# First pair of heads on one core: projections woven with the feed-forward's last down products, Q's and K's rests formed by VectorE, the other element's layer norm spread

## The reference

```python
# feed-forward: silu gate, RMS norm, down product
h  = silu(gate) * up
hn = rms_norm(h)                       # x * rsqrt(mean(x*x) + eps)
x  = x + 0.5 * einsum('bsh,dh->bsd', hn, wq_p)
# attention over the layer norm of x
qkv = einsum('bsd,od->bso', layernorm(x), w_qkv)
q, k = rope(q), rope(k)                # x*cos + rotate_half(x)*sin
attn = softmax(einsum('bqhd,bkhd->bhqk', q, k) / sqrt(128))
x = x + einsum('bso,do->bsd', einsum('bhqk,bkhd->bqhd', attn, v), w_out)
```

## Time and profile before

| what | value |
|---|---|
| median of 3 runs | 1762.09 us (1761.56 to 1762.62) |
| the profiled execution's own time | 1760.51 us |
| its span | 1758.7 us |
| PE busy | 1645.4 us, 94% of the span |
| DVE busy | 1287.1 us, 73% |
| ACT busy | 1219.9 us, 69% |
| POOL busy | 1126.1 us, 64% |
| mean granted TensorE clock | 0.991 |

### The profile page before, as it was taken

One profiled execution on the slowest core, in us unless ns is written; L12 is line 12 of the kernel. 1 busy time (PEld: TensorE's weight loads), 2 busy tenths in 40 slices (PEclk: granted clock), 3 DMA queues, 4 the chain that ended last, 5 costly groups with the idle time before them and its releaser, 6 DMA issues.

```text
span 1758.7 us, 26693 instructions
## 1 busy us (share of the span) xinstructions
PE 1645.4 (94%) x9307; PEld 963.8 (55%) x9307; DVE 1287.1 (73%) x2427; ACT 1219.9 (69%) x1886; POOL 1126.1 (64%) x747
## 2 busy tenths in 40 slices
PE   0898789999999999999999999998999999899998
PEld 0565345555555555555555555554565565676565
DVE  7877657777777777767777777786687778886766
ACT  6655778888888888988988888874654443325432
POOL 0554768888888888888888878883763222653222
PEclk9999899999999999999999999999999999999999
DMA  8100567887888878889878788784001210000001
GB/s 284 49 1 19 101 115 144 139 138 144 150 150 146 147 140 154 148 135 164 144 136 152 130 145 151 128 137 89 0 1 58 64 40 1 1 1 28 28 10 48
DMA packets 580506, 174.03 MB, mean 99 GB/s; under 512 B 543243, under 2 KB 579350, under 8 KB 580246
## 3 DMA queue, kind: packets, MB, share of 16 engines
q1 hardware_dynamic: 580374, 172.33, 51.8%
HBM read 35.94 MB, written 2.10 MB: 22 GB/s over the span
## 4 chain that ended last, share of the span: by engine, by line
PE 73%; DVE 8%; POOL 2%; issue 2%; ACT 1%; SPq 0%; DMA 0%; DVEq 0%; POOLq 0%; ACTq 0%
PE banks L1789 23%; PE banks L1790 23%; PE banks L1791 23%; DVE X L1644 1%; POOL sq_sum L684 1%; DVE mo_h L1631 1%; DVE nmax L1463 1%; DVE x L1196 1%; PE banks L1887 1%; PE banks L1855 1%; PE banks L1888 1%; PE banks L1856 1%; PE banks L1939 0%; PE banks L1799 0%; PE banks L2100 0%
## 5 line engine op out<-in xcount | busy, mean ns | idle before, releaser
L737 POOL TENSOR_TENSOR Pl<-Pm,Ph 128x1024 f16<-128x1024 f32 x256 | 546.4, 2134 | 52.3 <-ACT Ph L962 51.3
L952 ACT ACTIVATE Pm<-banks,nbias,s_scale 128x1024 f32<-128x1024 f32 x256 | 308.0, 1203 | 135.9 <-DVE nbias L1465 135.7
L1463 DVE TENSOR_REDUCE nmax<-banks 128x1 f32<-128x1024 f32 x256 | 312.6, 1221 | 111.6 <-PE banks L1791 110.5
L962 ACT ACTIVATE Ph<-Pm 128x1024 f16<-128x1024 f32 x256 | 268.3, 1048 | 1.2
L716 POOL TENSOR_TENSOR rp_b<-rp_s,rope 128x512 f32<-128x512 f32 x128 | 162.8, 1272 | 150.9 <-ACT rp_s L929 150.9
L1502 DVE SCALAR_TENSOR_TENSOR X<-banks,rinv,X 128x256 f32<-128x256 f32 x256 | 112.7, 479 | 156.8 <-PE banks L1791 156.8
L790 POOL TENSOR_TENSOR mT_lo<-mo_h,mT_hi 128x512 f16<-128x512 f32 x72 | 83.7, 1162 | 214.2 <-ACT mT_hi L1064 213.9
L1789 PE MATMUL banks<-QK_hi 128*128 128x512 f16 x512 | 197.1, 385 | 6.8 <-DVE QK_lo L1539 2.7
L1789 PE MATMUL banks<-PT_hi,V_hi 128*128 128x512 f16 x512 | 194.9, 381 | 3.2 <-DMA PT_lo<-Pl 3.2
L1790 PE MATMUL banks<-QK_lo,QK_hi 128*128 128x512 f16 x512 | 195.5, 382 | 0.0
L1791 PE MATMUL banks<-QK_hi,QK_lo 128*128 128x512 f16 x512 | 195.5, 382 | 0.0
(11 more groups left out here) (240 smaller groups left out, 4136.4 us busy)
## 6 DMA issues: line engine op xcount, KB each, us to landing
moe_raw<-in_L_ffn_W SPq DMA_DIRECT2D x72, 128.0 KB, 2.3
w_all<-in_L_attn_w_qkv SPq DMA_DIRECT2D x3, 2048.0 KB, 16.5
a_raw<-in_L_attn_w_qkv SPq DMA_DIRECT2D x24, 256.0 KB, 3.1
PT_hi<-Ph SPq DMA_TRANSPOSE x256, 3.4
PT_lo<-Pl SPq DMA_TRANSPOSE x256, 3.4
raw_gu<-in_L_ffn_w_gate_up SPq DMA_DIRECT2D x2, 1024.0 KB, 7.3
X<-in_L_attn_x SPq DMA_DIRECT2D x2, 1024.0 KB, 13.1
o_raw<-in_L_attn_w_out SPq DMA_DIRECT2D x8, 256.0 KB, 3.4
```

The source lines that it names most:

```text
L737: nc.gpsimd.tensor_tensor(Pl[:, z % 4, :], Pm[:, k, :], Ph[:, z % 4, :], ALU.subtract).then_inc(pl_done.sem, 1)
L952: nc.scalar.activation(Pm[:, k, :], two_banks[z % 2][:], ACT.Exp, bias=nbias[:, z:z + 1], scale=s_scale[:], accum_out=rsum[:, z:z + 1]).th ...
L962: nc.scalar.activation(Ph[:, z % 4, :], Pm[:, (base * SLOTS + z) % 3, :], copy).then_inc(ph_done.sem, 1)
L1463: nc.vector.tensor_reduce(nmax[:, z:z + 1], two_banks[z % 2][:], AX, ALU.max, negate=True).then_inc(max_done.sem, 1)
```

## The change

TensorE no longer finishes the four last down products before the projections. `ffn(0, 0)` returns two functions, the last phase's down product j and its squares, and `attention` calls them in this order: down 0, projections 0 and 1, squares, projection 2, down 1, projection 3, values 0, down 2, values 1, down 3, the first half scores. The banks change with it (downs 7, 6, 7, 6, squares 6, values 1 and 2), the wait for element 0's second normalised half stands ahead of down 0, the second half score waits for the second value rest, and the sides 0 and 1 of the first pair wait for the adds of down 3 and down 2. VectorE does the adds between its rope instructions; VectorE and ScalarE mix the weight copies with the last feed-forward ones.

All of Q's and K's rests of the first pair for its own heads (numbers 3 to 7) move from GpSimd to VectorE: number 3 behind the maximum of slot 0, a side's rest two slots after it, behind that slot's maximum. The variances of element 1 move from before the first maximum into slots 0 and 1, GpSimd's roots into its slots 1 and 2, and the normalising goes by two tiles in slots 1 to 4. Some buffers get other places in SBUF, so that attention's Q, K and V can be written while the last down products still read their operands.

```diff
@@ -244,15 +245,15 @@
     place["at"] = phase0
-    PT_hi = sb("PT_hi", [P, 2, TT, HALF], fp16)
-    PT_lo = sb("PT_lo", [P, 2, TT, HALF], fp16)
+    Pl = sb("Pl", [P, 4, S], fp16)
+    place["at"] = hT_at
     QK_hi = sb("QK_hi", [P, 2, 2, S], fp16)
     QK_lo = sb("QK_lo", [P, 2, 2, S], fp16)
+    PT_hi = sb("PT_hi", [P, 2, TT, HALF], fp16)
     V_hi = sb("V_hi", [P, 2, TT, 2 * HD], fp16)
     V_lo = sb("V_lo", [P, 2, TT, 2 * HD], fp16)
+    PT_lo = sb("PT_lo", [P, 2, TT, HALF], fp16)
     Ph = sb("Ph", [P, 4, S], fp16)
-    Pl = sb("Pl", [P, 4, S], fp16)
-    rp_q = sb("rp_q", [P, 2, HALF], f32)
     place["at"] = max(place["at"], top_ffn)
@@ -300,7 +302,8 @@
     N_POOL_LO = len(POOL_LO)
-    END_BANKS = [(4, 6, 7, 5), (4, 2, 3, 5)]
+    END_BANKS = [(7, 6, 7, 6), (4, 2, 3, 5)]
+    END_SQUARES = [6, 5]
@@ -352,8 +355,8 @@
     SIDES["first"] = {
-        0: [Side("qk", 0, 4, 6, ("v", 0, 1))],
-        1: [Side("qk", 0, 5, 7, ("v", 0, 0))],
+        0: [Side("qk", 0, 4, 6, ("ffn", 0, 3))],
+        1: [Side("qk", 0, 5, 7, ("ffn", 0, 2))],
         2: [Side("qk", 0, 6, 6, ("qk", 0, 4))],
@@ -750,14 +753,16 @@
                             rope_sine(side.i, c)
+                    if body == "first" and s in (1, 2):
+                        rsqrt_ln(1, 1, s - 1)
                     if s:
...
                     if has_slots(body):
-                        if s == 0 and body == "first":
-                            rope_lo(3, of)
                         for side in sides_of(s - 3):
+                            if body == "first" and side.d == 0:
+                                continue
                             rope_lo(side.i, lambda sig, i, d=side.d: of(sig, i, d))
@@ -772,8 +777,6 @@
                     rope_sine(j, pre, PRE_QKO)
-                for half in range(NHALF):
-                    rsqrt_ln(1, 1, half)
                 attention_pair("first", 0)
@@ -901,12 +904,15 @@
                         ln_hi(0, l + 1, ht // 4)
-                hi(NS - 1)
-                square(NS - 1)
                 if f == 0:
-                    for i in range(3):
-                        weights_hi(W_ORDER[i], bank[i], w_psum.in_head(0, i + 1))
+                    weights_hi(W_ORDER[0], bank[0], w_psum.in_head(0, 1))
+                    hi(NS - 1)
+                    weights_hi(W_ORDER[1], bank[1], w_psum.in_head(0, 2))
+                    square(NS - 1)
+                    weights_hi(W_ORDER[2], bank[2], w_psum.in_head(0, 3))
                 else:
+                    hi(NS - 1)
+                    square(NS - 1)
                     expert_weights_hi(0)
@@ -1026,15 +1032,15 @@
                 rope_shift_step(1, bank[0], pre(qk_psum, 2))
-                values_hi(0, 0, bank[7], pre(v_psum, 1))
                 rope_hi(0, pre(rope_sum, 1), PRE_QKO)
-                rope_hi(1, pre(rope_sum, 2), PRE_QKO)
-                values_hi(0, 1, bank[6], pre(v_psum, 2))
                 act.wait_ge(rope_b.sem, pre(rope_b, 1))
                 rope_shift_step(2, bank[4], pre(qk_psum, 3))
+                rope_hi(1, pre(rope_sum, 2), PRE_QKO)
                 act.wait_ge(rope_b.sem, pre(rope_b, 2))
                 rope_shift_step(3, bank[5], pre(qk_psum, 4))
+                values_hi(0, 0, bank[1], pre(v_psum, 1))
                 rope_hi(2, pre(rope_sum, 3), PRE_QKO)
+                values_hi(0, 1, bank[2], pre(v_psum, 2))
                 attention_pair("first", 0)
@@ -1348,7 +1354,7 @@
                     tiles = slice(phase % NHALF * TPH, (phase % NHALF + 1) * TPH)
-                    nc.vector.tensor_scalar(ms4[:, tiles], bank[5][:, D:D + TPH], 4.0 / FF, 4 * RMS_EPS, ALU.mult, ALU.add).then_inc(ms_ready.sem, 1)
+                    nc.vector.tensor_scalar(ms4[:, tiles], bank[END_SQUARES[f] if phase == len(PHASES) - 1 else 5][:, D:D + TPH], 4.0 / FF, 4 * RMS_EPS, ALU.mult, ALU.add).then_inc(ms_ready.sem, 1)
@@ -1412,17 +1418,21 @@
                         late_scales()
+                if f == 0:
+                    weights_lo(W_ORDER[0], bank[0], w_hi_done.in_head(0, 1))
+                    lo(NS - 1)
+                    weights_lo(W_ORDER[1], bank[1], w_hi_done.in_head(0, 2))
+                    add(len(PHASES) - 2, 3)
+                    weights_lo(W_ORDER[2], bank[2], w_hi_done.in_head(0, 3))
+                    mean_squares(len(PHASES) - 1)
+                    return (lambda j: add(len(PHASES) - 1, j))
                 lo(NS - 1)
                 add(len(PHASES) - 2, 3)
-                if f == 0:
-                    for i in range(3):
-                        weights_lo(W_ORDER[i], bank[i], w_hi_done.in_head(0, i + 1))
-                else:
-                    expert_weights_lo(0)
+                expert_weights_lo(0)
                 mean_squares(len(PHASES) - 1)
                 for j in range(TPH):
                     add(len(PHASES) - 1, j)
-                    if f and j == 1:
+                    if j == 1:
                         expert_weights_lo(1)
@@ -1449,6 +1459,12 @@
                 nc.vector.tensor_tensor(rp_q[:, j % 2, :], src, rp_b[:, j % 2, :], ALU.add).then_inc(rope_sum.sem, 1)
+
+            def first_rope_lo(j):
+                k = (PRE_QKO if j < 4 else QKO)[j % 4]
+                part = (slice(None), j // 4, k // 2, slice(k % 2 * HALF, (k % 2 + 1) * HALF))
+                dve.wait_ge(qk_hi.sem, qk_hi.in_pair(0, j + 1))
+                nc.vector.tensor_tensor(QK_lo[part], rp_q[:, j % 2, :], QK_hi[part], ALU.subtract).then_inc(qk_lo.sem, 1)
@@ -1507,6 +1523,12 @@
                         maximum(s)
+                    if body == "first" and s == 0:
+                        first_rope_lo(3)
+                    if body == "first" and s >= 2:
+                        for side in SIDES["first"][s - 2]:
+                            if side.name == "qk" and side.d == 0:
+                                first_rope_lo(side.i)
                     if body == "tail" and block_done(s, body):
@@ -1521,41 +1543,37 @@
                             add_head(side)
-                    if body == "first" and s in (1, 4):
-                        ln_normalise(1, 1, (1, 4).index(s))
+                    if body == "first" and s < NHALF:
+                        ln_variance(1, 1, s)
+                    if body == "first" and 1 <= s <= 4:
+                        ln_normalise(1, 1, (s - 1) // 2, range((s - 1) % 2 * 2, (s - 1) % 2 * 2 + 2))
                     if body == "last" and s == 7:
...
-            def attention():
+            def attention(last_down):
                 def pre(sig, i):
                     return sig.in_pair(0, i)
-                def rope_lo(j):
-                    k = PRE_QKO[j]
-                    part = (slice(None), 0, k // 2, slice(k % 2 * HALF, (k % 2 + 1) * HALF))
-                    dve.wait_ge(qk_hi.sem, pre(qk_hi, j + 1))
-                    nc.vector.tensor_tensor(QK_lo[part], rp_q[:, j % 2, :], QK_hi[part], ALU.subtract).then_inc(qk_lo.sem, 1)
-
                 dve.wait_ge(rope_in.sem, 16)
                 rope_cos(0, bank[3], pre(rope_shift, 2), PRE_QKO)
+                last_down(0)
+                rope_add(0, bank[3], pre)
                 rope_cos(1, bank[0], pre(rope_shift, 4), PRE_QKO)
-                rope_add(0, bank[3], pre)
                 rope_add(1, bank[0], pre)
-                values_lo(0, 0, bank[7], pre(v_hi_done, 1))
-                rope_lo(0)
-                rope_lo(1)
+                first_rope_lo(0)
                 rope_cos(2, bank[4], pre(rope_shift, 6), PRE_QKO)
-                dve.wait_ge(qk_lo.sem, pre(qk_lo, 1))
+                last_down(1)
+                first_rope_lo(1)
                 rope_add(2, bank[4], pre)
-                rope_lo(2)
-                values_lo(0, 1, bank[6], pre(v_hi_done, 2))
                 rope_cos(3, bank[5], pre(rope_shift, 8), PRE_QKO)
-                dve.wait_ge(qk_lo.sem, pre(qk_lo, 2))
+                values_lo(0, 0, bank[1], pre(v_hi_done, 1))
+                first_rope_lo(2)
                 rope_add(3, bank[5], pre)
-                for half in range(NHALF):
-                    ln_variance(1, 1, half)
+                values_lo(0, 1, bank[2], pre(v_hi_done, 2))
+                for j in (2, 3):
+                    last_down(j)
                 attention_pair("first", 0)
@@ -1862,7 +1879,7 @@
                     for j in range(TPH):
-                        last = nc.tensor.matmul(bank[5][:, D + j:D + j + 1], sq_sum[:, phase % NHALF, (FT - 1) % 2, j * P:(j + 1) * P], ones,
+                        last = nc.tensor.matmul(bank[END_SQUARES[f] if phase == len(PHASES) - 1 else 5][:, D + j:D + j + 1], sq_sum[:, phase % NHALF, (FT - 1) % 2, j * P:(j + 1) * P], ones,
                                                 start=True, stop=True)
@@ -1871,11 +1888,9 @@
                         to = bank[END_BANKS[f][j]]
-                        if j == 1 and f == 0:
-                            x_ready(0, l + 1, 1)
-                    if n >= 2 and (phase < len(PHASES) - 1 or j == 0):
```

(39 more changed lines are left out.)

8 lines of the change are left out of this document (4 added, 4 removed).

## The result

Before: 1761.56 us, median of 17 runs (1759.53 to 1762.76). After: 1765.83 us, median of 17 runs (1763.24 to 1769.32), ratio 1.0028 with a 95% interval of [1.002, 1.0035]. The change makes the kernel slower by 4.3 us in the medians and 4.9 us by the ratio; +6.4 was forecast. The profiled execution took 1769.25 us, with a span of 1767.5 at a mean granted clock of 0.986 (before: 1758.7 at 0.991).

A forecast was written before the change was run, and what follows sets the result against it. TensorE bounds from 280 us; before, the first head pair's ring through the engines does. Head start 5.7 spent in slots of 39.2 (+0.7), plus contention 5.7: +6.4 us, 1768.5 on the median of 1762.09; range 1761.5 to 1770.5.

The forecast's parts named there:

- The head start (5.7 us): First pair: the weaving lets the first row maximum start at about 164.2 us against 169.94, 5.7 us earlier.
- The rival in which the weaving stalls: VectorE late at the squares product or last value rest by 1 to 3 us: 1769.6 to 1772; chance 0.10.
- The slots: Seven slots of the first pair, first maximum to third values product: 39.2 us with nothing in VectorE's way.
- The count without contention: Slot times summing to 39.2 us; from 164.2 the third values product comes at 203.4 against 202.75, +0.7 us.
- the count with contention: The same slot times plus 5.6 to 5.7 us for VectorE instructions held up by GpSimd.
- the product: TensorE's third values product, where the count ends: 202.75 us before, forecast near 209.
- ring: First maximum to third values product, each slot passing through VectorE, ScalarE, GpSimd and TensorE; forecast 39.2 us without GpSimd interference.
- The idle times: VectorE idle ahead of its rests, waiting for ScalarE's QK_hi: about 3 us in slots 0, 2, 4; 2 in 3, 6.
- Contention (5.7 us): GpSimd delays VectorE's rests and normalised tiles in slots 0 to 4: 5.7 us, bounds nothing and 10.0.
- The rival of a small contention: GpSimd hardly delays VectorE: the sum falls to +0.7 to +3.5 us, 1762.8 to 1765.6; chance 0.20.
- Faster: Rival: the early start holds, seven slots under 35.0 us, time 1756.4 or 1758.6 us; chance 0.10.
- The sum (+6.4): Total at the third values product, +0.7 plus 5.7 us, carried unchanged to the kernel's end.

The follow-up runs named there:

- short_gpsimd: Changed kernel with GpSimd's sines and probability rests in the first pair's ring on 32 columns only; 1761.55 us against 1762.55 for the kernel before.
- rests_slot_later: Changed kernel with each VectorE rest one slot later, behind the next maximum; 1754.72 us against 1762.55 for the kernel before.
- rests_vector_only: Kernel before with only rests 3 to 7 moved to VectorE, no weaving, layer norm at its old places; 1767.1 us against 1762.55.
- the early variance: Changed kernel, rests one slot later, second variance behind the second maximum, four tiles in a row in slot 2; 1758.89 us against 1762.04 before.

## Why the prediction was right

**The head start (5.7 us)** was 5.5, or 6.1 counted from the weights' product. The adds, the cosines and the three early rests fitted beside the downs as counted, with 0.17 us of idle time ahead of the first maximum. The rival in which the weaving stalls is refuted.

**The slots.** All is in us, rounded. The count without contention against short_gpsimd, and the count with contention put into its slots against the changed kernel (from maximum to maximum, the last to the product):

| slot | 0 | 1 | 2 | 3 | 4 | 5 | 6 | sum |
|---|---|---|---|---|---|---|---|---|
| count | 6.1 | 4.3 | 7.5 | 6.6 | 6.7 | 2.9 | 5.0 | 39.2 |
| short_gpsimd | 6.1 | 4.2 | 7.4 | 6.5 | 6.6 | 2.9 | 5.2 | 38.7 |
| count with contention | 6.7 | 5.6 | 8.5 | 7.4 | 8.6 | 2.9 | 5.0 | 44.7 |
| after | 6.7 | 5.5 | 8.4 | 7.3 | 8.4 | 2.9 | 5.2 | 44.2 |

The mechanism is shown, not argued: with the wait moved one slot away (rests_slot_later) 11.6 us of ring are gone. The idle times came as named, 3.25 us in slots 0, 2 and 4 (about 3 forecast), 2.37 in slots 3 and 6 (2). The second exponential came 2.9 us earlier than before (172.59 for 175.47), not 3.5.

**Contention (5.7 us)** was 5.5. The rests of slots 0, 2 and 4 took 1.27 us, those without a sine beside them 0.69. By the rule of the Trainium skill's "SBUF — State Buffer", "Who interferes with whom", the rests should be blocked for the whole of GpSimd's instruction; these rows agree: the first sine ended at 169.86 and the rest at 170.41, 0.55 behind it (0.54 forecast). The rival of a small contention fell with short_gpsimd. The places of the single shares are sure for this kernel only: late, early and four-in-a-row tiles gave 1.4 to 5.2 us for the same work, which was my error in the expectations of rests_vector_only and of the early variance.

**Faster.** The rival needed a ring under 35.0 us; it was 44.2. The prediction asked for waits shorter by 0.9 in each of five slots, which holds only without contention; with the 5.5 us of it they would have had to be 1.8 shorter, and they were not shorter at all. But what spoke for it, a wait of 4.1 us for GpSimd's rest, was no bound either way: rings with GpSimd's rests (33.9) and with late VectorE rests (32.6) differ by 1.3 us. The Trainium skill's "GPSIMD Engine Reference", "4.1 Engine selection", would have the rest on VectorE; here the move cost where the rest's input was not there at its turn (1.0028 against 0.9965), and where it was, no gain over GpSimd is shown (0.9955 against 0.9965, with intervals that overlap).

**The sum (+6.4)** is the term that missed: +5.4 at the product from the weights' product on, close to it; +7.5 from 233 to 1219 us, since 1.6 us were lost to a stretch at 1.2 GHz behind the product, which the count took to be the last difference; and +4.2 to +4.3 in the medians. The first gap is shown by the windows in two profiles. So the lag at 1206 us was 1.2 us above the forecast and the medians 2.1 below it; the count covered neither what lies behind the product nor the end, and that the two pull opposite ways is luck. The second gap is not settled, but the profiles tell where it arises. From 290 to 1206 us every profile keeps its distance from that of the kernel before to within 0.4 us; between 1206 and 1278 us it changes, by +1.5 us in eight of the twelve, by -1.7 in three and by -0.1 in one, whatever was edited. The profile before is of an execution that was 1.05 us faster than that kernel's median (1760.51 against 1761.56), the first one after of one that was 3.4 us slower than its own, and spells at 1.2 GHz such as the one at 1220 us fall into some executions and not into others, 1.7 us each; no run shows how they are spread over the runs without a profile.

## What to carry to other kernels

An instruction in an ordered queue is priced by when its input arrives, not by its length alone: a 0.69 us subtraction was placed straight behind a maximum, while ScalarE forms its input only behind the exponential of that same maximum, and five of the seven slots waited for the round trip. One slot later the ring was 32.6 us, no longer than with GpSimd's rests (33.9). When parts of a change are bundled, the sum can hide a good one; here the weaving alone was worth -0.25%, and the whole change with its rests a slot later -0.45%. Place short VectorE work on SBUF operands where GpSimd is idle, and price it anew whenever the ring's pace changes. Neither bunching nor spreading it is better by itself: the eight tiles took 3.95 us four in a row and 6.35 two by two with the rests at once, but 8.10 and 3.33 with the rests a slot later (where in return the second variance took 3.36, not 0.77).

## What the runs showed of the hardware

The same four normalised tiles (128x256 each) took 1.37 us with GpSimd idle beside them and 5.22 with three of its instructions back to back; by these numbers about one tile came out behind each, an estimate, since the row gives only the four together. A whole variance, 0.77 us alone, took 3.36 us (171.73 to 175.09) beside two of GpSimd's. And behind one and the same wait of 3.1 us TensorE's granted clock over the next products (1220 to 1224 us) was 0.57 in one execution of the program and 1.00 in another, worth 1.7 us.
